# Diffusion block on one core: two groups of maximum pieces, and an order of items for each engine

## The reference, cut to what matters

```
h = layernorm(x) * (1 + ca) + sa
q = h @ Wq  (16 heads of 64),  k = h @ Wk,  v = h @ Wv  (4 heads of 64)
q = q * cos + rotate_half(q) * sin;  k likewise
attn = softmax(q k^T / 8)            per head, 512 x 512
x = x + ga * ((attn v) @ Wo)
```

## Time and profile before

| | us |
|---|---|
| median of 3 runs | 1281.28 (1279.19 to 1281.62) |
| profiled execution | 1279.61 |
| its span, first to last instruction | 1277.8 |
| first C of the first pair to first C of the last pair | 54.8 to 815.4 |
| last matmul of the first attention | 845 |
| granted share of PE's clock, mean | 0.953 |

### The profile page before, as it was taken

How to read it: one execution, slowest core, us unless ns; L and a number is a source line. 1 busy time by engine, 2 the same in 40 slices (tenths; PEclk the granted TensorE clock), 3 DMA queues, 4 the chain that set the end, 5 groups by cost and what they waited for, 6 DMA issues and landing times. The chain is left out here.

```text
span 1277.8 us, 30408 instructions
## 1 busy us (share of the span) xinstructions
PE 1119.9 (88%) x11049; PEld 708.2 (55%) x11049; DVE 1003.6 (79%) x1484; ACT 650.3 (51%) x1284; POOL 901.5 (71%) x744
## 2 busy tenths in 40 slices
PE   3689999989999998999999999766887989897975
PEld 2245565555565564565564565454544666665854
DVE  4588968967977976877877879746858999998884
ACT  2245545634545544645645645425765655554442
POOL 3388878867879877869878969612437797877721
PEclk9699999999999998999999999977987999999998
DMA  5212212112112112112111211110000000000000
GB/s 150 50 39 52 48 30 52 46 34 52 39 27 64 39 27 51 42 39 51 40 39 43 47 39 37 38 30 0 1 2 0 1 1 1 1 9 10 9 17 25
DMA packets 48726, 42.21 MB, mean 33 GB/s; under 512 B 7973, under 2 KB 46904, under 8 KB 48568
## 3 DMA queue, kind: packets, MB, share of 16 engines
q1 hardware_dynamic: 48136, 39.35, 12.8%
q10 hardware_dynamic: 432, 0.79, 0.2%
HBM read 6.42 MB, written 2.10 MB: 7 GB/s over the span
## 5 line engine op out<-in xcount | busy, mean ns | idle before, releaser
L505 ACT ACTIVATE a_probs<-a_ps_s 128x512 f32<-128x512 f32 x512 | 303.9, 597 | 325.9 <-PE a_ps_s L417 321.4
L736 POOL TENSOR_TENSOR a_p_lo<-a_probs 128x512 f16<-128x512 f32 x384 | 420.1, 1116 | 32.8 <-ACT a_probs L505 29.6
L664 DVE TENSOR_REDUCE a_nmx<-a_ps_m 128x2 f32<-128x1024 f32 x256 | 311.1, 1216 | 32.7 <-PE a_ps_m L400 31.8
L433 PE MATMUL a_ps_o<-a_v_hi,a_probs 128*128 128x65 f16 x2048 | 243.7, 196 | 16.1 <-DVE a_p_lo L671 8.4
L434 PE MATMUL a_ps_o<-a_v_lo,a_probs 128*128 128x64 f16 x2048 | 241.0, 194 | 0.0
L435 PE MATMUL a_ps_o<-a_v_hi,a_p_lo 128*128 128x65 f16 x2048 | 240.7, 195 | 0.0
L433 PEld LDWEIGHTS a_ps_o<-a_v_hi,a_probs 128*128 128x128 bf16 x2048 | 189.9, 99 | 88.1 <-issue 58.7
L415 PE MATMUL a_ps_s<-a_qq,a_kk 128*128 128x512 f16 x512 | 197.3, 385 | 9.3 <-issue 6.3
L434 PEld LDWEIGHTS a_ps_o<-a_v_lo,a_probs 128*128 128x128 bf16 x2048 | 191.6, 99 | 25.0 <-issue 1.3
L417 PE MATMUL a_ps_s<-a_qq,a_k_l 65*128 65x512 f16 x512 | 198.0, 387 | 0.0
L435 PEld LDWEIGHTS a_ps_o<-a_v_hi,a_p_lo 128*128 128x128 f16 x2048 | 191.2, 98 | 0.0
(11 more groups left out here) (238 smaller groups left out, 2130.8 us busy)
## 6 DMA issues: line engine op xcount, KB each, us to landing
a_qq<-a_rhi SPq DMA_DIRECT2D x128, 128.0 KB, 2.4
a_qq<-a_rlo SPq DMA_DIRECT2D x128, 64.0 KB, 2.0
a_kk<-a_rhi SPq DMA_DIRECT2D x64, 64.0 KB, 2.0
a_k_l<-a_rlo SPq DMA_DIRECT2D x32, 64.0 KB, 2.0
out_x<-x_sb SPq DMA_DIRECT2D x8, 256.0 KB, 2.3
a_qq<-a_nmT SPq DMA_DIRECT2D x64, 2.0 KB
a_probs<-in_wq ACTq DMA_DIRECT2D x1, 512.0 KB, 5.0
a_wo<-in_wo SPq DMA_DIRECT2D x1, 512.0 KB, 11.9
```

The lines of the kernel that those rows point to most:

```text
L433: nc.tensor.matmul(out, hi, v_hi[:, b % 2, kt, g, 0:65], start=(kt == 0), stop=False)
L505: nc.scalar.activation(probs[:, p % 2, kt, h, :], ps_s[:, i % 2, :], ACT.Exp, scale=DH0 ** -0.5).then_inc(exp_done, 1)
L664: nc.vector.tensor_reduce(nmx[:, p % 2, i:2 * QT:QT], ps_m[:, n % 2, :, :], axis=X, op=ALU.max, negate=True).then_inc(free[n % 2], 1)
L736: nc.gpsimd.tensor_tensor(p_lo[:, p % 2, kt, h, :], pr, pr.bitcast(BF16)[:, 1:2 * L:2], ALU.subtract).then_inc(lo_pool, 1)
```

## The change

`pipeline()` with its slots goes. `first_order(engine)` builds a list for each engine from tables: an item of pair p stands at tick 32 p + place, an item of sequence b at 256 b + place, and items are sorted by tick, then by the order of `KINDS`. A step is 32 ticks, so that slot k of before answers to ticks 4 k. PE's order numbers the jobs and the buffers of the rotated parts (`rope`, by A and K instead of RS and KS). The loop stays.

On PE a plain step of 32 ticks now reads: C0, B0, B1, D, D, C1, C2, A, D, M, C3, D, C4, B2, B3, D, C5, D, C6, O, D, C7, D. The orders of the others follow the same tables. Among what moves: MX behind exp 1, M on SP to tick 5, A on DVE behind the first division, W on PE from behind C0 to the end of the step before it, LN 2 on DVE behind W, both KL of POOL and SP into the step after the K step.

```diff
-def pipeline():
...
-        if pair(s + 2):
-            for i in range(4):
-                slots[2 * i].append(("B", s + 2, i))
-        if pair(s + 3):
-            slots[1].append(("A", s + 3))
-            slots[3].append(("RS", s + 3))
-            slots[4].append(("RH", s + 3))
-            slots[5].append(("RL", s + 3))
...
+PAIR_AT = {
+    "PE": {"C": (0, 4, 8, 12, 16, 20, 24, 28), "B": (-64, -64, -48, -48), "A": (-88,), "M": (-21,), "O": (88,), "D": (24, 28, 32, 35, 40, 44, 48, 52)},
+    "ACT": {"C": (0, 4, 8, 12, 16, 20, 24, 28), "RH": (-80,), "MX": (-28,), "M": (-20,), "O": (90,)},
+    "DVE": {"A": (-88,), "B": (-64, -64, -48, -48), "L": (6, 10, 14, 18, 19, 24, 26, 34), "D": (16, 28, 29, 32, 38, 41, 45, 49)},
+    "POOL": {"RS": (-87,), "RL": (-80,), "L": (1, 5, 13, 14, 20, 29, 32, 32)},
+    "SP": {"RL": (-78,), "M": (-27,)},
+}
+SEQ_AT = {
+    "PE": {"HT": (-172,), "K": (-152, -139), "V": (-108,), "W": (317,)},
+    "ACT": {"HT": (-172,), "KH": (-140, -132), "V": (-106,)},
+    "DVE": {"LN": (-203, -193, -193), "K": (-152, -140), "V": (-108,), "W": (316,)},
+    "POOL": {"LN": (-208, -205, -202), "HL": (-176,), "KS": (-143, -135), "KL": (-120, -119), "W": (324,)},
+    "SP": {"KL": (-120, -120)},
+}
...
+def first_order(engine):
+
+    items = []
+
+    def put(tick, it):
+        items.append((tick, len(items), it))
+
+    for kind in KINDS:
+        for i, at in enumerate(PAIR_AT[engine].get(kind, ())):
+            for p in range(B * PAIRS):
+                put(32 * p + at, (kind, p) + ({"C": (i,), "B": (i,), "L": (i,), "D": divmod(i, QT)}.get(kind, ())))
+        for i, at in enumerate(SEQ_AT[engine].get(kind, ())):
+            for b in range(B):
+                put(256 * b + at, (kind, b) + ((i,) if kind in ("LN", "K", "KS", "KH", "KL") else ()))
+    for tick, it in ONCE_AT[engine]:
+        put(tick, it)
+    steps = {s: [] for s in range(FIRST, LAST + 1)}
+    for tick, _, it in sorted(items, key=lambda x: x[:2]):
+        steps[tick // 32].append(it)
     return steps
...
-    steps = pipeline()
+    order = {e: first_order(e) for e in ("PE", "ACT", "DVE", "POOL", "SP")}
...
-        for it in steps[s]:
+        for it in order["PE"][s]:
             if it[0] in ("A", "K", "B", "M", "O", "V", "HT", "W", "G", "FT"):
                 job[it] = len(job)
-            if it[0] in ("RS", "KS"):
+            if it[0] in ("A", "K"):
                 rope[it[1:]] = len(rope)
...
-        def run(eng, item):
+        def run(eng, name, item):
+            steps = order[name]
```

More of the change, by code:

```diff
@@ new lines @@
+PAIR_AT = {
[5 rows of a table added]
+}
+SEQ_AT = {
[5 rows of a table added]
+}
+ONCE_AT = {
[7 rows of a table added]
+    "POOL": (),
+    "SP": ((1980, ("FL",)),),
+}
+KINDS = ("C", "W", "B", "A", "RS", "RH", "RL", "MX", "M", "O", "D", "L", "LN", "HT", "HL", "K", "KS", "KH", "KL", "V")
+def first_order(engine):
[14 more added lines that the diff above has]
+        steps[tick // 32].append(it)
@@ L132, in layer0_attention @@
                 rope[it[1:]] = len(rope)
     ropes_in_order = list(rope)
-    JOBS16 = job[("O", LOOP_FROM - 2 + PERIOD)] - job[("O", LOOP_FROM - 2)]
-    ROPE16 = rope[(LOOP_FROM + 3 + PERIOD,)] - rope[(LOOP_FROM + 3,)]
+    JOBS16 = job[("O", 1 + PERIOD)] - job[("O", 1)]
+    ROPE16 = rope[(6 + PERIOD,)] - rope[(6,)]
     assert JOBS16 % 2 == 0 and ROPE16 % 2 == 0
@@ L343, in item @@
                         sp.dma_start(f_w[f][:, 6 * D:FW], names[2]).then_inc(ld_f, 16)
-            run(sp, item)
+            run(sp, "SP", item)
         @block.tensor
@@ L465, in item @@
                     last.then_inc(full[n % 2], 1)
-            run(pe, item)
+            run(pe, "PE", item)
         @block.scalar
@@ L533, in item @@
                                          ps_m[:, n % 2, :, 0:INNER], ACT.Copy).then_inc(free[n % 2], 1)
-            run(act, item)
+            run(act, "ACT", item)
         @block.vector
@@ L692, in item @@
                     quantize(*it[1:])
-            run(dve, item)
+            run(dve, "DVE", item)
         @block.gpsimd
@@ L741, in item @@
                     nc.gpsimd.tensor_tensor(x_seq(t, b), x_seq(t, b), yg[:], ALU.add).then_inc(x_done, 1)
-            run(pool, item)
+            run(pool, "POOL", item)
 KB, NB = D // BLK, INNER // BLK
```

## The result

| | before | after |
|---|---|---|
| median | 1280.78 (1279.19 to 1281.62) | 1250.08 (1246.55 to 1250.46) |
| ratio, 95% interval | | 0.9756 (0.9735 to 0.9776) |
| profiled execution, its span | 1279.61, 1277.8 | 1246.55, 1244.7 |
| first C of pair 0, of pair 63 | 54.77, 815.4 | 55.77, 786.7 |
| from there to the last instruction | 462.4 | 458.0 |

A forecast was written before the change was run, and what follows sets the result against it. PE was taken as the bound, at 98% of a plain step. Terms -18.3 - 4.3 - 9.8 - 0.7 - 7.0 - 0.2 + 2.0 = -38.3 from 1279.6 gave 1241.3, median 1243.0; range 1234 to 1268.

The forecast's parts named there:

- Plain steps: The 28 ordinary steps of the first attention: 10.12 to 9.64 us, by 0.30 of tile-shape changes and a 0.16 wait saved.
- Rival 1: On PE, the second B of a group pays its own weight load, 0.10 each: +12.2, 1255 us; chance 0.15.
- DVE keeps up: In a plain step of 9.64 us, DVE just fits: 9.28 of own work and one wait of 0.3.
- Rival 3: POOL's RS starts before DVE's L2, which takes 1.95; steps of 10.35, 1292 us; decides at 3.1 for both L; chance 0.08.
- The V step: Seven steps with V: D no longer waits for POOL's L7, since both KL move later; -9.8 us, bounds 0 and -10.8.
- the list of signs: The prediction's closing list of what would show it, such as V step near 11.0, K 12.6, first C at 56.5.
- HT and W: Steps starting a coming sequence (HT) and ending a finished one (W): shorter waits on PE, -1.0 × 7 = -7 us.
- mode changes: PE's switches of tile shape around B and M: 0.30 us saved per step over 61 steps, -18.3.
- First steps: The first three steps, which waited 4.4 us on reductions: 2 us given back.
- K steps: Seven steps with K: shorter waits of K0, remaining waits of K1 and D; together -0.1 × 7 = -0.7 us.
- The first C: C0 of pair 0, at the start of the attention: 1.8 us later, since K DMAs and the first B start later.
- slips: Allowance of +2 us over the whole attention, because DVE's slack is only about 0.04 to 0.3.

The follow-up runs named there:

- Run 2: Changed kernel with the four B of a pair spread to four places again (-64, -56, -48, -40) on PE and DVE; 1294.94 us, ratio 1.0131.
- run 7: Changed kernel with DVE's L2 moved behind the third piece's reduction (place 16, fourth B at -47); 1268.84 us, ratio 0.9913.
- run 4: Changed kernel with V later: PE at -104 instead of -108, ACT and DVE at -101, behind L on DVE; 1269.06 us, ratio 0.9923.
- Run 9: Changed kernel with POOL's KL computing only half of its columns from the second sequence on, work left out; 1249.62 us, ratio 0.9756.
- Run 6: Changed kernel with both KL of POOL back in the K step (-136 and -131 instead of -120 and -119); 1258.14 us, ratio 0.9818.
- Run 3: Changed kernel with LN2 on DVE at -197 instead of -193, ahead of W's part instead of behind it; 1237.90 us, ratio 0.9678.
- run 1: Kernel before, with its one shared list of slots: B grouped in slots 0 and 4, M moved from slot 4 to 2; 1339.37 us, ratio 1.0473.

## Why the prediction was right, and where it was off

**Plain steps: right.** 9.64 was forecast and 9.64 measured. The unknown prices, both taken from far rows, came out as taken: a piece behind a piece 0.22 (0.215 taken, from the gate matmuls), M's way in about 0.10 (0.095 taken). Rival 1, the second weight load at 0.10, is out: with it the four-matmul row would show 0.64 to D and not 0.54, and the loads' row shows them done while the first piece's matmuls run. The Trainium skill, TensorE: Matmul & The Clock Gate, Part 3, The mechanism, says that a weight load overlaps running matmuls only when its row group differs, and both pieces use the same row groups; these rows disagree. Run 2 takes back four changes of tile shape, at 0.46 a step, with 0.06 in it that lies between the first two matmuls of O, which there stands right behind a piece. The Trainium skill, TensorEngine Tiling (Array Packing), Key Properties, says that a change of tiling mode drains the engine; a price of 0.10 for each change agrees with that.

**DVE keeps up: right, for a better reason than mine.** I had it just fit at 9.28 of work, with L2 and L6 at 1.46 and 1.11. They take 0.68 each, so DVE idles 1.4 us a step. Rival 3 turned on who starts first, L2 or RS; L2 does, as argued. The two L together take 1.37 us, and the rival decides from 3.1, so it was never near in plain steps. What L2 costs when it stands right behind RS no run shows: run 7 put a reduction between them.

**The V step: right in sign, short by 0.5.** By the sum it would take 11.2 (12.90 less 1.4 and 0.3; the list of signs says 11.0), and it takes 11.67: 3.4 us over seven sequences. The term that was mis-sized is the end of POOL's L3. The prediction had it at 9.4 to 9.8 of the step and D at 9.78, and said that PE pays if POOL is later by 0.5. L3 ends at 10.28 and D starts at 10.52, 0.24 behind it: POOL comes out of the K step without idle time, and RS, taken to end at 7.2, ends at 8.17. At the same time DVE's L2 took 1.62 beside POOL, and the reduction behind it holds V, whose matmuls stand in front of D, by 0.5. The two delays lie side by side, so that taking away one of them gains nothing: run 4 takes V's wait away, and D starts no earlier. Run 9 relieves both, and the step takes 11.10. Run 6 shows that moving both KL is worth the 8 us, but not by the wait named: with KL early PE waits for an exp in front of C, and not at D for L7.

**HT and W: the term that failed.** -7.0 was forecast beside the mode changes, +3.1 measured by the same account (-1.1 in all, of which -4.2 are mode changes). The step is named in the prediction: LN2 behind DVE's W, "1.1 us", holding PE's A by 0.56. LN2 took 2.81, since L and W of POOL run beside it, and A waited 1.93: six times 1.37, 8.2 us of the 10.1. The prediction took it seven times, but the last W has no LN2 behind it. I had copied the 1.12 of the earlier trace rows from a place where POOL stood still. A second, small one: the second piece behind W waits 0.3 for DVE to read W's buffer (174.18, 0.92 for four matmuls instead of 0.61), seven times, 2 us. Run 3 removes the first and gains 12 us, more than the whole gap of the forecast.

**First steps.** I gave 2 us back and they cost 1.7. Most of it is the same cause: LN2 of the second sequence starts behind POOL's rstd, has four operations of 1 us each, beside POOL, and A behind it waits 5.3 us. The granted clock is at the lower level from 81.5 to 88.3, from inside that wait on (in before from 83.7 to 87.1):

```profile
79.14 4.05 DVE L616 TENSOR_SCALAR a_xhat<-x_sb,a_mv,a_rstd 128x128 f32<-128x128 f32 x4 [1.19 <-POOL a_rstd L688]
```

The first C comes 1.0 later, not 1.8; why, no run tells.

**Errors that helped.** K steps gained 0.66 and not the 0.4 of the sum (which makes 12.9; the list of signs says 12.6), and the two steps at each loop edge 1.8 us more between them than their like elsewhere (before 4.5 and 1.6 above them, after 3.1 and 1.2). Why, no run tells. The last four steps and what stands behind them gave 6.7 us that I had at 0.6: 2.3 in the steps, 2.2 in the drain of the last pair (granted clock 0.88 there, 0.79 in before), and 2.2 in the feed-forward part, whose code is unchanged, 1.3 of them in its first 30 us and nearly all in its first 50. There the granted clock differs (PEclk is the column of 0.89 and 0.77; the first 15 us behind W of after, then the next 15):

```profile
815.00:830.00 15.00, 7.44 (x18) 2.91 (x18) 2.99 (x19) 6.03 (x14) 3.97 (x6) 0.89 0.23 63
830.00:845.00 15.00, 8.31 (x27) 4.83 (x27) 6.85 (x21) 7.21 (x15) 2.27 (x3) 0.77 0.00 0
```

In before the two stretches that answer to them (845 to 860, 860 to 875) show 0.77 and 0.66, and a matmul of 512 columns there took 1.05 us in the median, 0.61 in after. From the last pair's first C to the end all kernels with the tables take 457.5 to 460.1 us, before and the kernel of run 1 462.4 and 462.5. I read it as the clock being granted earlier behind a shorter attention; that the clock differs is shown, why is not.

So the profiled execution came out 5.3 us above the forecast's 1241.3: +10.1 from HT and W, +3.4 from V, +4.6 from the first three steps; less 2.0 of slips, 3.0 of K, 1.0 in plain steps, 0.8 of the first C and 6.1 at the end (the rest is rounding). The size was right in the total because misses of both signs met, which is luck, and in the plain steps because the prices were.

## What to carry to other kernels

Where matmuls of one tile shape stand alone between those of another, putting them side by side saved about 0.2 us for each that was joined here, and the followers (reduction, copy, DMA) have to be placed with it: done in a shared list, as run 1 did it, it cost 4.7%. The duration of a DVE or POOL operation belongs to its place as much as to the operation: before moving one, look at what the other engine runs there, and put what must be moved into a wait that exists anyway (LN2 into the 6 us of W: 1%). Price the rare steps as carefully as the common one: here the common one was exact, and nearly all of the error was in the others.

## What the runs showed of the hardware

- DVE's 128x128 layernorm operation (LN2) takes 0.34 us in the median before and 0.70 after, up to 1.30, for the same instructions (engine, count, shortest, median and longest duration in ns; after, then before):

```profile
L616 DVE TENSOR_SCALAR a_xhat<-x_sb,a_mv,a_rstd x32: 335/702/1302, 14.4 to 649.6; 128x128 f32 x24, 128x128 f32<-128x128 f32 x8
```

```profile
L641 DVE TENSOR_SCALAR a_xhat<-x_sb,a_mv,a_rstd x32: 335/344/1076, 14.3 to 663.7; 128x128 f32 x24, 128x128 f32<-128x128 f32 x8
```

  Four short ones beside POOL's chain of operations cost some 1.0 each (79.14, 4.05 for four), as if each waited for the end of one of POOL's (1.04). The Trainium skill, SBUF — State Buffer, section SBUF: two separate sides, describes a lock held for a whole instruction; this agrees, and it makes many short operations the worst neighbours.
- The lock costs the other side too: RS on POOL 1.27 alone, 1.64 behind an L of DVE that started 0.16 earlier.
- Changing the tile shape costs PE about 0.10 us each way, for 64-row pieces and for the 8-column M; a 64-row piece behind another costs its columns alone (0.22), and its weight loads run under the matmuls in front of it.
- Behind a wait of PE of 1.77 us the granted clock fell from 1.00 to 0.50 (368.2 to 371.6) in one of six steps with the same wait, in three of six in run 6 and two of six in run 9; it cost the step another 1.55 us.
